# Scores and exponentials of an attention issued by sides of two banks, in a four-layer model planned anew (one Trainium2 core)

## What is computed

```python
x = x + xattn_l(layernorm(x), ctx)      # l = 0..2: 16 heads of 16, softmax over 154 keys
x = x + ffn_l(layernorm(x))
# ffn 0: ternary weights, squared relu;  ffn 1: product-key experts, 32 of 4096 rows a token
# gathered, beside a gated MLP;  ffn 2: top 2 of 8 gated experts and shared ones
# layer 3: autocorrelation attention, then top 2 of 8 linear experts
scores = jnp.einsum('bthd,bshd->bhts', Q, K) / jnp.sqrt(DH)
P = jax.nn.softmax(scores, axis=-1)
out = jnp.einsum('bhts,bshd->bthd', P, V).reshape(B, T, D) @ Wo + b_o
```

## Time and profile before

| | |
|---|---|
| median of 3 runs | 1609.88 us |
| the profiled execution | 1606.96 us |
| its span, first to last instruction | 1605.2 us |
| TensorE busy | 1290.2 us, 80% |
| VectorE busy | 1102.5 us, 69% |
| ScalarE busy | 811.9 us, 51% |
| GpSimd busy | 692.4 us, 43% |
| mean granted clock of TensorE | 0.885 of 2.4 GHz |

### The profile page before, as it was taken

How to read it: one execution, slowest core, us unless ns; L and a number is a source line. 1 busy time by engine, 2 the same in 40 slices (tenths; PEclk the granted TensorE clock), 3 DMA queues, 4 the chain that set the end, 5 groups by cost and what they waited for, 6 DMA issues and landing times.

```text
span 1605.2 us, 18853 instructions
## 1 busy us (share of the span) xinstructions
PE 1290.2 (80%) x5862; PEld 655.7 (41%) x5862; DVE 1102.5 (69%) x2945; ACT 811.9 (51%) x2053; POOL 692.4 (43%) x705
## 2 busy tenths in 40 slices
PE   4999997766779777678657676776889999999998
PEld 2345453233244434333323533442444444544544
DVE  5642418589987886998899988898863334436455
ACT  2454442756757876747557568558735341130200
POOL 2000000488888888846878778888400010010000
PEclk9799898877789889778669699989999999989999
DMA  6000000466575758634657866655310031002000
GB/s 232 24 1 0 10 1 8 86 179 162 164 165 176 196 162 222 162 106 128 176 158 172 227 167 185 180 167 167 90 24 1 0 126 34 0 27 74 1 14 27
DMA packets 59957, 168.68 MB, mean 105 GB/s; under 512 B 15760, under 2 KB 20944, under 8 KB 59216
## 3 DMA queue, kind: packets, MB, share of 16 engines
q0 software_dynamic: 40960, 134.25, 31.5%
q1 hardware_dynamic: 18896, 33.22, 6.4%
HBM read 162.61 MB, written 4.82 MB: 104 GB/s over the span
## 4 chain that ended last, share of the span: by engine, by line
PE 42%; POOL 21%; DVE 19%; issue 10%; ACT 4%; DMA 3%; SPq 0%; DVEq 0%; POOLq 0%; ACTq 0%
POOL bufR L1881 18%; PE psum L1210 7%; PE psum L1072 5%; PE psum L1084 3%; POOL half_sum L1895 3%; PE psum L1154 2%; PE psum L1129 2%; DVE bufB L1568 2%; DMA bufR<-in_table,rowid 2%; PE psum L820 2%; PE psum L1007 2%; DVE bufR L1440 2%; PE psum L954 2%; PE psum L999 2%; DVE x_sb L1458 1%
## 5 line engine op out<-in xcount | busy, mean ns | idle before, releaser
L1881 POOL DMA_INDIRECT bufR<-in_table,rowid x512 | 559.1, 1092 | 227.9 <-issue 121.3
L1235 ACT ACTIVATE bufR<-bufR 128x256 f32<-128x256 f32 x512 | 205.5, 405 | 61.2 <-DVE bufR L1440 60.7
L1440 DVE TENSOR_TENSOR bufR<-bufR 128x1024 f32<-128x1024 f32 x128 | 161.2, 1262 | 53.7 <-DMA bufR<-in_table,rowid 53.5
L1072 PE MATMUL psum<-xtf,wf 128*128 128x512 f32 x320 | 153.0, 622 | 16.0 <-DVE x_sb L1734 13.1
L1244 ACT ACTIVATE bufR<-bufR,ew 128x256 f32<-128x256 f32 x128 | 63.8, 504 | 133.6 <-DVE ew L1448 133.5
L1503 DVE TENSOR_TENSOR x_sb<-x_sb,psum 128x256 f32<-128x256 f32 x128 | 50.6, 416 | 115.7 <-PE psum L1007 69.0
L858 PE MATMUL psum<-bufB 32*128 32x308 f32 x576 | 71.2, 571 | 63.7 <-DVE bufB L1568 50.0
L1908 POOL TENSOR_TENSOR x_sb<-x_sb,wattn 128x256 f32<-128x256 f32 x16 | 11.1, 728 | 254.9 <-DMA wattn<-in_attn 147.7
L1901 POOL TENSOR_TENSOR x_sb<-x_sb,wattn 128x256 f32<-128x256 f32 x32 | 22.7, 741 | 220.4 <-DMA wattn<-in_attn 140.4
L1841 DVE SCALAR_TENSOR_TENSOR x_sb<-psum,bufR,x_sb 128x256 f32<-128x256 f32 x128 | 61.9, 483 | 74.6 <-PE psum L1210 69.8
L1084 PE MATMUL psum<-wf,bufR 128*128 128x256 f32 x320 | 84.1, 411 | 34.3 <-DVE bufR L1725 34.3
(11 more groups left out here) (240 smaller groups left out, 2528.5 us busy)
## 6 DMA issues: line engine op xcount, KB each, us to landing
bufR<-in_table,rowid POOLq DMA_INDIRECT x512, 4.3
wf<-in_ffn SPq DMA_DIRECT2D x2, 2304.0 KB, 14.9
bufR<-in_ffn SPq DMA_DIRECT2D x1, 2696.5 KB, 16.8
wattn<-in_attn SPq DMA_DIRECT2D x4, 641.0 KB
wf<-in_rope SPq DMA_DIRECT2D x4, 512.0 KB, 6.2
bufB<-in_ffn SPq DMA_DIRECT2D x1, 2048.0 KB, 8.4
scr_corr<-bufR SPq DMA_DIRECT2D x16, 128.0 KB, 2.3
bufR<-scr_corr SPq DMA_DIRECT2D x4, 512.0 KB, 4.6
```

The source lines that it names most:

```text
L1072: ins = mm(bank(6 + r), gu[:, kt, r, :], xtf[:, kt, :], start=kt == 0, stop=kt == KT - 1)
L1235: own.mark(act(row, row, ACT.Identity, accum_out=dots[:, g % 4, j:j + 1]))
L1440: tt(rows, rows, cast(xg[c % 2][:, i, :].unsqueeze(1), [P, GRP, D]), ALU.mult).then_inc(f1_mu, 1)
L1881: eng.indirect_dma_start(ring[:, s * GRP + j, :], None, io["table"], bass.IndirectOffsetOnAxis(ap=rowid[c % 2][:, at + j:at + j + 1], axis ...
```

## The change

It splits each round s into two items, sh (g, par, side): two products of float32 and two of bfloat16 into two banks, with a semaphore and an exponential each. A side of the second round waits only for the exponential of its own banks, the rest r only for side 0 of the second round, the first side of the second group no longer for the copies of the values, and an exponential of the second group only for the product w that read its side. A product w waits for its own rest. The turn-back t (G) waits for its own copy and may stand beside the last products w. The offsets PREFER are new, and with them the order on every engine.

```diff
-    PE=dict(kv=3.9, X=1.45, Q=4.1, p1=1.0, ph=0.45, mt=0.7, s=1.6, r=1.5, w=2.4, t=0.5, o=0.75, y=1.1, h0=2.0, y0=3.7, q1=4.6, sm1=1.25,
+    PE=dict(kv=3.9, X=1.45, Q=4.1, p1=1.0, ph=0.45, mt=0.7, sh=0.85, r=1.5, w=2.4, t=0.5, o=0.75, y=1.1, h0=2.0, y0=3.7, q1=4.6, sm1=1.25,
...
-    ACT={("gu1",): -100, ("gu1", 3, 1): 380, ("r",): 230, ("s",): 15, ("sc",): 85},
+    ACT={("N2", "a"): 145, ("N4",): -55, ("gu1", 3): -45, ("r", 2): -115, ("sc",): 155, ("sh", 0, 2, 0): -100, ("w", 2, 1, 1):
+        -45},
...
-                p = pe("s", 1.6, last, g and on("ACT", "w", 0), g and on("ACT", "w", 1), n=(g, par))
-                last = add("ACT", ("s", layer, c, g, par), 2.1, p)
-            p = pe("r", 1.6, last, n=(g,))
-            last = add("ACT", ("r", layer, c, g), 1.4, p)
+                for side in range(2):
+                    if par:
+                        free = (on("ACT", "sh", g, 0, side),)
+                    elif g:
+                        free = (on("ACT", "w", 0), on("ACT", "w", 1)) if side else (last,)
+                    else:
+                        free = (last,)
+                    p = pe("sh", 0.8, *free, n=(g, par, side))
+                    add("ACT", ("sh", layer, c, g, par, side), 1.1, p, g and on("PE", "w", side))
+            p = pe("r", 1.6, on("ACT", "sh", g, 1, 0), on("PE", "sh", g, 1, 1), n=(g,))
+            last = add("ACT", ("r", layer, c, g), 1.4, p, on("ACT", "sh", g, 1, 1))
...
-            p = pe("t", 0.6, on("ACT", "w", G4 - 1 if G >= 2 else G), w, G and on("PE", "t", G - 1), n=(G,))
-            add("DVE", ("t", layer, c, G), 0.9, p)
+            p = pe("t", 0.6, on("ACT", "w", G), last, G and on("PE", "t", G - 1), n=(G,))
+            add("DVE", ("t", layer, c, G), 0.9, p, on("PE", "w", 2))
...
+                if par:
+                    eng.wait_ge(at_ex, 12 * k + 6 * g + side + 1)
+                elif g:
+                    eng.wait_ge(at_ex, 12 * k + 6)
+                    if side:
+                        eng.wait_ge(at_ou, 4 * k + 2)
...
-                for z in range(BANDS):
+                for z in (2 * side, 2 * side + 1):
                     mm(bank(z), keysm[band(z), g, b, par, 0:P], q[band(z), g, :], start=True, stop=False)
-                for z in range(BANDS):
+                for z in (2 * side, 2 * side + 1):
                     ins = mm(bank(z), sel[band(z), 2 * g + par, :], mt[band(z), :], start=False, stop=True)
...
-                eng.wait_ge(at_ex, 12 * k + 6 * g + 4)
+                eng.wait_ge(at_ex, 12 * k + 6 * g + 3)
...
-                eng.wait_ge(at_ex, 12 * k + 6 * (G // 2 + 1))
+                eng.wait_ge(at_ex, 12 * k + 6 * (G // 2) + 5 + G % 2)
...
-                eng.wait_ge(at_ou, 4 * k + G + 1 if G < 2 else 4 * k + 4)
+                eng.wait_ge(at_ou, 4 * k + G + 1)
...
+                eng.wait_ge(at_pv, 4 * k + 3)
                 eng.wait_ge(at_tt, 4 * k + G + 1)
```

More of the change, by code:

```diff
@@ L1294, in turn_max, with score @@
                 if k:
-                    eng.wait_ge(at_s2, 6 * k)
+                    eng.wait_ge(at_s2, 10 * k)
                 eng.wait_ge(at_mt, k + 1)
                 act(mt[:, :], bank(0), ACT.Copy).then_inc(at_mts, 1)
-            def score(layer, c, g, par):
+            def score(layer, c, g, par, side):
                 k = chunk(layer, c)
                 if g:
-                    eng.wait_ge(at_pv, 4 * k + 2)
+                    eng.wait_ge(at_pv, 4 * k + side + 1)
                 elif k:
                     eng.wait_ge(at_wo, TI * k)
-                eng.wait_ge(at_s2, 6 * k + 3 * g + par + 1)
-                for side in range(2):
-                    act(probs[side][:, par:4:2, :], psum[:, 2 * side:2 * side + 2, :], ACT.Exp).then_inc(at_ex, 1)
+                eng.wait_ge(at_s2, 10 * k + 5 * g + 2 * par + side + 1)
+                act(probs[side][:, par:4:2, :], psum[:, 2 * side:2 * side + 2, :], ACT.Exp).then_inc(at_ex, 1)
             def score_rest(layer, c, g):
                 k = chunk(layer, c)
-                eng.wait_ge(at_s2, 6 * k + 3 * g + 3)
+                eng.wait_ge(at_s2, 10 * k + 5 * g + 5)
                 for side in range(2):
@@ L1420, in _ @@
             work = {"th": gathered_sums, "sc": weighted_rows, "N2": deviation, "N4": norm, "X": transposes, "Q": project,
-                    "kv": kv, "mt": turn_max, "s": score, "r": score_rest, "w": weigh, "o": turn_out, "tern": tern, "h0": hidden0, "q1": queries1, "gu1": gate1, "tk1": top1,
+                    "kv": kv, "mt": turn_max, "sh": score, "r": score_rest, "w": weigh, "o": turn_out, "tern": tern, "h0": hidden0, "q1": queries1, "gu1": gate1, "tk1": top1,
                     "lg2": logits2, "gu2": gate2_up2, "K3": keys3, "V3": values3, "q3": q3, "co": corr, "tp": top, "o3": out3,
@@ L1542, in kv @@
                 if layer:
-                    eng.wait_ge(at_s2, 6 * (chunk(layer - 1, 2 * b + 1) + 1))
+                    eng.wait_ge(at_s2, 10 * (chunk(layer - 1, 2 * b + 1) + 1))
                 for par in range(PAR):
```

28 lines of the change are left out of this document (11 added, 17 removed).

## The result

| | before | changed | ratio (95% interval) |
|---|---|---|---|
| median | 1609.88 us (4 runs) | 1622.63 us (4 runs, 1620.06 to 1623.47) | 1.0075 (1.0057 to 1.0092) |
| profiled execution | 1606.96 us | 1623.15 us | |
| its span | 1605.2 us | 1621.4 us | |

What follows compares the result with a forecast made beforehand. It took TensorE to bound the kernel up to 300 us and from 1139 on, GpSimd's gathers between. Gains of 12.8 + 0 + 0.2 = 13 us from 1609.9 gave 1597 us, range for 8 in 10 1583 to 1611.

Steps and rivals of the forecast that it cites:

- The middle: Gathers up to chunk 2's row numbers: 3.4 us more VectorE work against shorter attention waits, net 0 (-6 to +6).
- Half of those 28.5 us may go: All twelve attentions: TensorE's waits for exponentials shrink by about half, 14 us over the program, most under the gathers.
- Attention (0,0): Ahead of the first gather: the new order ends its last addition earlier, gain 10 us (4 to 12).
- Tern and N3: Ahead of the first gather: X earlier in (0,1), +1.5 us (0 to 2), and in (1,0), +5 (3 to 6.4).
- Lone sides: In (0,1) and (1,0), TensorE full: two extra groups each at 1.28 us, -4 us (-5.1 to -1.3).
- First gather 287.5: Sum of the parts ahead of the gathers, 12.8 us (2 to 21): first gather near 287.5 instead of 300.3 us.
- Rival 2: TensorE score sides: neighbouring sides don't overlap, eight groups per attention instead of four; 1615 us (1609 to 1621), chance 0.12.
- Rival 1: Pause before chunk 2: gathers start 13 us earlier but row numbers come as late as now; 1609 us, chance 0.10.
- The gathers behind 731: Third stage, 731 to 1139 us: no reason for a change in the gathers' pace.
- The bounds of the sum: Whole kernel: the bounds of the parts add to -7 and +31 us; ahead of the first gather 2 to 21.
- The tail: Last 466 us: earlier Q against one extra group in (2,3) and a few waits, +0.2 us (-3 to +4).

Runs made afterwards that it cites:

- a3: Changed kernel's code with the order of the kernel before up to the first gather and behind the last, new order only between; ratio to before 1.0088.
- a4: Changed kernel's code with the new order up to the first gather and behind the last, order of the kernel before between; ratio to before 0.9983.
- d1: Changed kernel's code with the new order only from the first gather to the end of attention (1,2), old order elsewhere; ratio to the kernel before 1.0093.
- d2: As d1, but the first pass of attention (0,2) is in the old order too; ratio to the kernel before 1.0063.
- a1: Changed kernel's split and waits, but every engine in the order of the kernel before, each round's two sides next to each other; ratio to before 0.9992.
- b5: Changed kernel's code, new order to the first gather with sides of (0,1) and (1,0) together, old order behind; 1603.27 us in a single execution.
- c4: Changed kernel's code with the new order only from the end of attention (1,2) to the last gather, old order elsewhere; ratio to the kernel before 0.9977.
- a2: Changed kernel, own order, but on TensorE and ScalarE each side 0 stands right before its side 1; ratio to the kernel before 1.0075.
- b2: Changed kernel with GpSimd's bias additions of (0,2) and (1,3) issued one by one behind four gathered units; ratio to the kernel before 1.0042.
- c2: As b5, with GpSimd's bias additions of (0,2), (0,3), (1,2) and (1,3) issued one by one behind gathered units; ratio to the kernel before 0.9907.
- c3: Changed kernel with the old-order first pass of (0,2), as in b1, and bias additions in pieces, as in b2; ratio to the kernel before 1.0029.
- b1: Changed kernel with the old order from the first gather to the end of the first pass of (0,2); ratio to the kernel before 1.0036.

## Why the prediction was wrong, point by point

- **"The middle: net 0 (-6 to +6)" is the step that failed.** It measured +16.5 us between the two traces. The forecast counted the VectorE work that stands ahead of the row numbers of chunk 2 (one more unit, 3.4 us) and set shorter waits against it. It didn't follow the attentions of the middle item by item on three engines. The path to the row numbers goes through (0,2), (0,3) and (1,2), and in the new lists it meets waits that the trace of before doesn't have, 6.44 us at r of (0,2) and up to 5.3 us for a feed-forward product, and two VectorE additions of 4.01 us. Where the order showed it was not costed: on VectorE the four turn-backs of (0,2) stand behind the products of 23 to 25 gathered units instead of 22, those of (0,3) behind 40 instead of 37. That this stretch makes the loss is shown (a3, a4, d1, d2); which of its waits makes how much of it is not.
- **"Half of those 28.5 us may go": nothing measurable.** a1 has the shorter waits (between 300 and 760 us 7.3 us ahead of scores instead of 12.1, and 5.1 ahead of r instead of 8.8) and the ratio 0.999.
- **Attention (0,0), "10 (4 to 12)": 4.0.** The last addition starts at 85.64 instead of 89.64, at the low bound. The clock rose where the text wanted it, 0.53 to 0.91 between 61 and 79 us. Part of what is missing is chance: the changed kernel came to its first scores 2.1 us later (42.41 against 40.29), with the same list on TensorE and a lower clock. But the gain is small in the other traces too: the last addition of (0,0) starts at 87.91 to 89.64 in the seven with the old order there and at 83.88 to 85.87 in the six with this one, sides of (0,1) and (1,0) apart. The new order also left gaps behind the turn-backs.
- **Tern and N3: right in kind.** X of the front in (0,1) comes 5.9 us earlier, 1.9 more than the additions (+1.5 forecast). X in (1,0) starts at 170.30 instead of 179.99, 5.3 more than the end of (0,1); the forecast had 6.5 gross:

```profile
168.27 2.10 PE L882 MATMUL psum<-bufB 32*128 32x308 f32 x8 [1.57 <-DVE bufB L1584]
170.30 1.97 PE L817 MATMUL psum<-const,xa 128*128 128x128 f32 x8
```

- **Lone sides, -4: about right.** b5 gives 3.5 us for the four, the steadier measure above some 4. In attention (1,0), from this X to the start of its last output projection, it took 68.3 us instead of 61.1: three pairs of first-pass units (2.2), two lone sides (2.6), and some 2.5 that remain, mostly new gaps of 0.5 to 1.5 us, which the forecast didn't have. So a lead of 9.7 us at X became 2.5 at the end of the attention.
- **First gather 287.5: it was 298.9.** Of 12.8 us 1.5 came: 6 are missing in (0,0), the rest in the gaps and in leads that the next stage used up. Here the trace of before is a fast one of its kind: the seven traces with the old order have the first gather at 300.3 to 303.0, the six with the new one at 297.4 to 298.9. All of that gain is made in (0,0); from its last addition on, the old order takes 210.7 to 214.1 us and the new one 212.9 to 213.5. The forecast had 2.8 us for this part.
- **Rival 2, neighbouring sides don't overlap: false**, 1.29 us a pair; with a second product into the same bank the pair is still no longer than a round. The sentence of the Trainium skill on program order ("TensorE: Matmul & The Clock Gate", section "The mechanism") is not borne out here: all eight float32 records of the pair at 188.93 start before the first of the four bfloat16 ones at 189.89, those of the second side too. The 2.19 us of a pair whose second side must wait, named in the forecast as a sign of this rival, are no such sign.
- **Rival 1, the pause eats it: seen in part**, and it had too little chance. In a4 the gathers begin 1.8 us earlier than in a1 and the pause ends 0.9 later; in b5 they begin 5.3 earlier and it ends 2.1 earlier. It named the place that decides (VectorE 96% busy ahead of the row numbers), but only as a limit on the gain; that the attentions of the middle could come later and turn it into a loss, no rival had.
- **The gathers behind 731, "nothing reasons for a change":** 4.8 us more in the two profiles, and of this kind wherever the new order stands there (c4).
- **The bounds of the sum.** The parts ahead of the first gather add to 1.2 and 19.7, not 2 and 21, and all parts to -7.8 and +29.7; rival 1 comes to 1609.7 us. Nothing hangs on it.
- **The tail, +0.2 (-3 to +4)**: -3.6 in the two profiles, and not to be told from none over the other runs.

## What to carry to other kernels

When an order is planned anew, follow the items on the path to the next thing waited for (here the row numbers of chunk 2) through every engine's new list, and put the durations and table loads of the trace on what now stands ahead of each; here the gain of a few waits could not be measured (a1), and the places of the attentions behind gathered work cost 0.9%. Test the mechanism and the order apart: the same code in the old order told in one run that the split was free and worthless, and halves of the list told where the loss was. A version with the old middle, the new front and the sides kept together there was faster than the kernel before: 0.991 on one chip, 0.994 in the single execution on another. And compare more than two traces: that of before had a clock in its first 61 us that none of the six others with the old front had.

## What the runs showed of the hardware

A VectorE addition with its inputs in SBUF can be held for as long as GpSimd's additions follow each other without a gap: 4.01 us beside five, 1.99 beside two, 0.48 alone. In other places the two engines take turns. In the kernel before, around 652 us, VectorE's three additions beside the same five of GpSimd:

```profile
650.91 0.84 DVE L1457 SCALAR_TENSOR_TENSOR x_sb<-bufR,ew,x_sb 128x256 f32<-128x256 f32 x1
651.78 0.84 DVE L1458 SCALAR_TENSOR_TENSOR x_sb<-bufR,ew,x_sb 128x256 f32<-128x256 f32 x1
652.65 0.83 DVE L1459 SCALAR_TENSOR_TENSOR x_sb<-bufR,ew,x_sb 128x256 f32<-128x256 f32 x1
```

There GpSimd's four take 3.40 us instead of 2.75. What decides between the two wasn't tried, but the traces have a pattern in who starts first. In all ten cases with a held addition (two each in the changed kernel, a2, a3, b2 and c2) it had started 0.25 to 0.35 us ahead of GpSimd's first. Six that had started 0.41 to 0.46 us ahead (a2, a3, c2, c3, d1 and the changed kernel, at 384.67) took 0.83 to 0.85 (a seventh, in b1, 1.51), and one that starts behind it, as here (650.91 after 650.67), takes its turn. The Trainium skill, page "SBUF — State Buffer", section "SBUF: two separate sides", says that whichever of the two engines starts first has the shared ports for its whole instruction and the other blocks. The turns agree with that. The long waits don't: VectorE's addition starts at 351.52 and GpSimd's first at 351.80, so VectorE should have been first, and at the latest its turn should have come behind one addition and not five.

Score sides of 32 rows overlap fully, also with two products into a bank, if both may start at once (1.29 us for two, 1.28 for one); then a side alone costs what two do. If the second starts 0.92 us late, the two take 2.19.
